# A four-batch transformer layer on one core: the instruction order of its 64 attention and feed-forward steps, and of the edges between batches, is changed

## The reference, cut to what matters

```
xn  = layernorm(x)
q, k, v = xn @ wq.T, xn @ wk.T, xn @ wv.T      # 8 heads, two maps (64 wide queries and keys) each
attn = softmax(causal(q1 k1)) - lambda * softmax(causal(q2 k2))
o   = attn @ v;  o = o * rsqrt(mean of o*o over groups of 8 + eps) * (1 - L_INIT);  att = o @ wo.T
h   = silu(xn @ W1.T) * (xn @ W3.T);  h = fwht(h);  ff = h @ W2.T
x   = x + att + ff                              # then layer 1: a recurrence and 64 routed experts
```

## Time and profile before

| | us |
|---|---|
| median of 3 runs | 3774.03 (3768.78 to 3781.55) |
| profiled execution: its time | 3770.78 |
| its span | 3769.0, mean granted clock 0.940 |
| PE busy | 3183.8 (84%) |
| DVE busy | 1951.8 (52%) |
| ACT busy | 1364.2 (36%) |
| POOL busy | 1859.7 (49%) |

### The profile page before, as it was taken

One profiled execution on the slowest core, in us unless ns is written; L12 is line 12 of the kernel. 1 busy time (PEld: TensorE's weight loads), 2 busy tenths in 40 slices (PEclk: granted clock), 3 DMA queues, 4 the chain that ended last, 5 costly groups with the idle time before them and its releaser, 6 DMA issues. The chain is left out here.

```text
span 3769.0 us, 46728 instructions
## 1 busy us (share of the span) xinstructions
PE 3183.8 (84%) x16049; PEld 2443.1 (65%) x16049; DVE 1951.8 (52%) x3951; ACT 1364.2 (36%) x2989; POOL 1859.7 (49%) x1707
## 2 busy tenths in 40 slices
PE   2899999899999979999989999995888983088776
PEld 0677777677777767777767777773776762044443
DVE  6355556645565655655664556565544655811110
ACT  2344444344444424444443444443323321022221
POOL 3256667646576645765773657654222241033333
PEclk9899999999999999999999999997998986589998
DMA  5211111321111141110123111103121111099897
GB/s 156 83 37 43 40 37 43 106 71 45 31 43 45 40 134 40 40 48 29 40 84 98 43 37 40 42 21 121 54 70 67 58 64 60 18 266 246 240 245 177
DMA packets 251183, 301.99 MB, mean 80 GB/s; under 512 B 19664, under 2 KB 168016, under 8 KB 250320
## 3 DMA queue, kind: packets, MB, share of 16 engines
q1 hardware_dynamic: 236624, 263.49, 22.3%
q0 software_dynamic: 14336, 35.66, 4.5%
HBM read 233.46 MB, written 65.57 MB: 79 GB/s over the span
## 5 line engine op out<-in xcount | busy, mean ns | idle before, releaser
L799 ACT ACTIVATE probs<-score_ps,neg_max 128x640 f32<-128x640 f32 (+7 forms) x512 | 374.4, 738 | 363.0 <-DVE neg_max L660 362.5
L690 POOL TENSOR_TENSOR probs<-probs 128x512 f32<-128x512 f32 (+3 forms) x384 | 383.4, 1013 | 10.7
L685 POOL TENSOR_SCALAR probs<-probs,comb 128x512 f32<-128x512 f32 (+3 forms) x384 | 230.0, 607 | 309.2 <-DVE comb L596 301.3
L660 DVE TENSOR_REDUCE neg_max<-score_ps 128x2 f32<-128x256 f32 (+7 forms) x256 | 346.5, 1353 | 58.9 <-PE score_ps L915 55.2
L694 POOL TENSOR_TENSOR out_root<-out_root,neg_half 128x16 f32<-128x16 f32 x128 | 371.8, 2907 | 5.7 <-DVE out_root L630 5.7
L552 DVE TENSOR_TENSOR layer_sum<-product_ps,layer_sum 128x512 f32<-128x512 f32 x384 | 262.4, 684 | 44.7 <-PE product_ps L61 41.6
L912 PE MATMUL score_ps<-keys_all,queries_all 64*128 64x512 f32 (+3 forms) x2304 | 277.2, 363 | 0.0
L539 DVE TENSOR_TENSOR attT<-turn_ps,attT 128x512 fp32r<-128x512 f32 (+3 forms) x384 | 211.6, 551 | 84.5 <-ACT attT L720 84.3
L720 ACT ACTIVATE attT<-turn_ps 128x512 fp32r<-128x512 f32 (+3 forms) x384 | 188.2, 490 | 142.8 <-PE turn_ps L825 142.8
L912 PEld LDWEIGHTS score_ps<-keys_all,queries_all 64*128 64x128 f32 x2304 | 187.8, 185 | 74.0 <-issue 44.7
L59 PE MATMUL product_ps<-xT_hi,w_up 128*128 128x512 f32 x512 | 211.6, 413 | 28.3 <-DVE queries_all L559 20.2
(11 more groups left out here) (248 smaller groups left out, 7676.3 us busy)
## 6 DMA issues: line engine op xcount, KB each, us to landing
e_gate_up<-in_w_gate_dram SPq DMA_DIRECT2D x64, 384.0 KB, 4.0
e_gate_up<-in_w_up_dram SPq DMA_DIRECT2D x64, 384.0 KB, 5.4
e_down<-in_w_down_dram SPq DMA_DIRECT2D x64, 384.0 KB, 6.8
w_stage<-in_wqk_dram SPq DMA_DIRECT2D x64, 256.0 KB, 3.1
w_stage<-in_w1T_dram SPq DMA_DIRECT2D x64, 256.0 KB, 2.6
w_stage<-in_w3T_dram SPq DMA_DIRECT2D x64, 256.0 KB, 2.7
values_by_head<-hidden_split SPq DMA_DIRECT2D x32, 512.0 KB, 3.2
w_stage<-w_transformed SPq DMA_DIRECT2D x64, 256.0 KB, 2.7
```

Source lines behind the costliest of these rows:

```text
L660: dve.tensor_reduce(nmax[:, i % 2, :], score_tile(i % NT), AX.X, ALU.max, negate=True)\
L685: pool.tensor_scalar(PR[:, r, 1, c], PR[:, r, 1, c], comb[:, i % 4:i % 4 + 1], 1.0, ALU.mult, ALU.mult)\
L690: pool.tensor_tensor(PR[:, r, 0, c], PR[:, r, 0, c], PR[:, r, 1, c], ALU.add).then_inc(s_comb, 1)
L799: act.activation(PR[:, i % 2, q, 0:(j + 1) * P], score_tile(j)[:, q, :], ACT.Exp, bias=nmax[:, i % 2, q:q + 1], accum_out=sums[:, i % 16, ...
```

## The change

It gives every engine a new order within a step, starts a batch's x earlier, and shortens the edges.

- TensorE: gate or up goes to the front of the step, ahead of values and the first turn; down goes from behind the scores to behind the turns; output goes ahead of projection (and so do their places in the bank order).
- ACT: tanh of gate goes to the front; the high part of a projection goes from the start of the next step, behind the weight copies, to directly behind this step's exponentials; the pair's high part goes behind the hidden tile's.
- DVE: output's sum goes to the front of the step, ahead of the projection's low part and the reciprocal; scaling of `heads_out` moves one step later, to its front; the factor of the normalised heads and the map's low part go behind gate or up; down's sum goes from the end of the step to before `comb`, and `comb` to directly before the pair's low part and the maximum.
- Edges: 11 slots instead of 13. Three tiles of x get a buffer of their own (`x_early`); they are loaded, and the first is prepared, in the last three steps of the batch before (slots -3 to -1, which run beside steps 61 to 63). Normalisation and statistics go to the end of a slot, transposes come in slots 1 to 8 (before 3 to 10), values in slots 2 to 9 (before 4 to 11).

```diff
-    HEAD_SLOTS, TAIL_SLOTS = 13, 10
+    HEAD_SLOTS, TAIL_SLOTS, EARLY = 11, 10, 3
+        XE = sb("x_early", [P, EARLY, D])
# phases()
-                for s in range(HEAD_SLOTS if b < batches else TAIL_SLOTS):
+                for s in range(0 if b else -EARLY, HEAD_SLOTS if b < batches else TAIL_SLOTS):
                     yield b - 1 if b else None, STEPS + s, b if b < batches else None, s
                 if b < batches:
                     for i in range(STEPS):
-                        yield b, i, None, None
+                        more = i >= STEPS - EARLY and b + 1 < batches
+                        yield b, i, b + 1 if more else None, i - STEPS if more else None
# SP
+                    if hb and s == -EARLY:
+                        sp.wait_ge(s_xtf, (hb - 1) * NT + EARLY)
+                        for t in range(EARLY):
+                            load_x(hb, t)
+                    if hb and s in (0, 1):
                         sp.wait_ge(s_ttf, tt[b, i, 1] + 1)
-                        for t in range(4 * s, 4 * s + 4):
+                        for t in range(EARLY + 4 * s, min(NT, EARLY + 4 * s + 4)):
                             load_x(hb, t)
# ACT
                     if b is not None:
-                        if proj_at(i - 1):
-                            proj_high(b, *proj_at(i - 1))
+                        if i < STEPS and i % 2 == 0:
+                            act.wait_ge(s_gbf, gb["GU", b, i] + 1)
+                            act.activation(sg[:, :], gbank("GU", b, i), ACT.Tanh, scale=0.5).then_inc(s_tanh, 1)
...
+                    if b is not None and proj_at(i):
+                        proj_high(b, *proj_at(i))
# TensorE
                     if b is not None:
+                        if i < STEPS:
+                            gate_up(b, i)
                         g = group_at(i)
                         if g is not None:
                             values(b, g)
                         if has_turn(i):
                             turn_map(b, i, 0)
-                    if hb is not None and 3 <= s < 3 + NT:
+                    if hb is not None and 1 <= s < 1 + NT:
...
-                        if i < STEPS:
-                            gate_up(b, i)
+                        if has_down(i):
+                            down(b, i)
...
-                        if has_down(i):
-                            down(b, i)
...
+                        if pair_at(i):
+                            output(b, i)
                         if proj_at(i):
                             project(b, *proj_at(i))
-                        if pair_at(i):
-                            output(b, i)
```

More of the change, by code:

```diff
@@ L612, in _ @@
-                        if has_turn(i):
-                            map_low(b, i, 0)
+                        g = group_at(i - 1) if i else None
+                        if g is not None:
+                            h = g // 4
+                            dve.wait_ge(s_ox, b * GROUPS + g + 1)
+                            if h % 2 == 0:
+                                at = (b, 16 * (h // 2) + g % 4 * 2 + 1, 2) if h else (b - 1, STEPS + g % 4 * 2 + 1, 2)
+                                if at[0] >= 0:
+                                    dve.wait_ge(s_ttf, tt[at] + 1)
+                            for q in range(2):
+                                tile = 2 * (g % 4) + q
+                                r = (h * NT + tile) % 16
+                                ins = dve.tensor_scalar(O[:, tile, h % 2 * DH:(h % 2 + 1) * DH],
+                                                        PV[:, 2 * P + q * DH:2 * P + (q + 1) * DH], rsum[:, r, 0:1], None, ALU.mult)
+                            ins.then_inc(s_oxf, 1)
@@ L749, in _ @@
                 for b, i, hb, s in phases():
-                    if hb is not None and 5 <= s < 5 + NT:
-                        t = s - 5
+                    if hb is not None and 3 <= s < 3 + NT:
+                        t = s - 3
                         act.wait_ge(s_vf, hb * NT + t + 1)
@@ L924, in _ @@
                             turn_map(b, i, 0)
-                    if hb is not None and 3 <= s < 3 + NT:
-                        t = s - 3
+                    if hb is not None and 1 <= s < 1 + NT:
+                        t = s - 1
                         pe.wait_ge(s_xn, hb * NT + t + 1)
```

164 lines of the change are left out of this document (76 added, 88 removed).

## The result

The changed kernel takes 3718.2 us (median of 4 runs, 3708.9 to 3721.6), the kernel before, measured beside it, 3774.6 (4 runs, 3768.8 to 3781.6). The ratio is 0.9846 with an interval of 0.9822 to 0.9870: 56 us, 1.5%, faster. The forecast was 3665 in a range of 3605 to 3735, so the time is inside the range, and the gain is about half of the 106 us that the sum gave.

The account below looks back on a forecast made before the run. TensorE's queue with a few holes was taken to bound the steps, chains the edges. Gains of 44 (steps), 37 (later edges) and 25 (first edge), 106 in all, took 3771 to 3665 us, range 3605 to 3735.

Parts of the forecast that it names:

- First edge, 25 us: Edge before the first batch: v(0) starts at about 93, slots of 3.4 instead of 6.86 us; gain 25 us.
- Later edges, 37 us: Three edges between batches: 74 us from the last maximum against 87.9, two slots dropped; gain 12.5 each, 37 in all.
- Last edge, 0 within 3: Edge after the last batch: slots stay at 3.6 us, down hides in that chain; change 0, within 3 us.
- Steps, 44 us: 64 steps in each of four batches: 25 - 11 - 3 = 11 us shorter, four times 44; bounds 0 and 100.
- 25 us of holes gone: Steps of a batch: TensorE's waits at values, up products and transposes, 18 to 25 us, taken as 25, all gained.
- 11 back at pair heads: New waits where pair heads start (fold, pair's transpose, later steps): 3.65 us for each of 3, 11 a batch.
- comb behind down's sum: In the steps: POOL's maps start later but keep 2.3 us of cover before the next turn; cost nothing.
- comb's holds, 3 a batch: In the 24 pair steps: comb held by a POOL copy beside it, between 0 and 1 us; 3 a batch.
- rival A: In the steps, holes only move: comb's holds and ACT's tanh cost all 25 us a batch; 3709 us, chance 0.24.
- C: In the steps, late comb makes a loop over POOL: 1.9 us for each of 96 pair steps, 182; 3891, chance 0.07.
- B: Edges bound by TensorE after slot 2 without clock loss, steps losing nearly all holes: 3594 us, chance 0.13.
- D: GpSimd's root holds the normalisation in edges (up to 2.4 us in 8 slots) and steps: 58 us, 3723, chance 0.03.

Follow-up runs that it names:

- Experiment 11: Changed kernel with comb directly behind the reciprocal and GpSimd's weight low parts in steps 15, 31, 47, 63 cut to 8 columns (work left out): 3664.5 us.
- experiment 1: Kernel before with only the changed edges, the order within steps left as before: 3722.7 us, ratio 0.9873.
- experiment 6: Changed kernel with comb directly behind the reciprocal and the mean again, ahead of down's sum: 3684.7 us, ratio 0.9766.
- experiment 5: Changed kernel with a projection's high part on ACT back at the start of the next step, behind the weight copies: 3722.7 us, ratio 0.9862.
- experiment 7: Changed kernel with GpSimd's weight low parts in steps 15, 31, 47, 63 cut to 8 of 512 columns, the rest left out: 3672.8 us.
- experiment 2: Changed kernel with 3 and 8 unread matmuls added before and behind the fold in steps 16, 32, 48: 3696.8 us, ratio 0.9803.
- experiment 8: Changed kernel with wo's piece at tile 4 of heads 1, 3, 5, tanh behind outT and map high, and DVE's factor, then map low first: 3744.2 us.
- experiment 3: Changed kernel with the output projection's weight piece handled at tile 4 of heads 1, 3, 5 instead of tile 7: 3684.5 us, ratio 0.9766.

## Why the prediction was half right

**What bounds the kernel: right.** TensorE's queue in the steps, chains in the edges. The holes named went away.

**First edge, 25 us: right (27.2).** v products start at 92.5, the first slot runs at half the pace until 96.5, and then slots come each 3.2 us (transposes at 100.46, 103.65, 106.86) against 6.86 before.

**Later edges, 37 us: right in kind, 30.1 measured.** Late slots with an output were put at 5.4 us; they take 5.32:

```profile
1318.74 0.60 PE L946 MATMUL score_ps<-ident_sb,probs 128*128 128x128 f32 x4
1318.84 2.91 POOL L705 TENSOR_TENSOR out_root<-out_root,neg_half 128x16 f32<-128x16 f32 x1
...
1320.09 0.28 DVE L618 SCALAR_TENSOR_TENSOR heads_out<-heads_out,out_root 128x128 f32<-128x128 f32 x1
...
1324.06 0.60 PE L946 MATMUL score_ps<-ident_sb,probs 128*128 128x128 f32 x4
```

The slots' sum gave 74 us from the last maximum. Experiment 11 has 74.5, at a clock of 0.98; the changed kernel has 77.7 to 79.3, at 0.89 in the row above, with stretches of 17.0 us at 1.2 GHz in the third edge where 3.4 are in experiment 11's. The term that failed is the 1.5 us "for clock at half in slots 0 and 1" with the waits in these slots; together they cost 3 to 5 us more per edge. How much of that is the clock was not run apart.

By stage the forecast asked for more than 37 here and for less in the steps: down of step 63, 1.4 us, moves into the steps (354 matmuls of down between the first and the last scores of a batch, 348 before). So by stage the forecast is 88 to 74 us an edge, 41.7 us in three, of which 30.1 came, and 38.4 us in the steps.

**Last edge, 0 within 3: wrong, 4.7 us longer.** With the old order of a step and the new edges it takes 41.6 us (experiment 1), so the new order makes it longer; with `comb` early it takes 43.6 (experiment 6). The rest is open.

**Steps, 44 us: wrong, 2.9 us longer instead.** This is the step of the prediction that failed, and its largest term. By its own terms:
- *25 us of holes gone.* The waits at up products and values went, as said. But by experiment 5 the eviction's place gives only 1 us in a head without pairs: the output ahead of the projection and gate or up in front had done the rest.
- *11 back at pair heads.* The chain was right (fold 0.5: measured 0.52; second turn 0.75: 0.48; pair 0.9: 0.72 in experiment 7). It left out that the factor, 0.28 us, can be held like `comb`; it took 1.39. The prediction had the row of a held `comb` (1.15 us) and applied it only to `comb`. The two copies that step 15 leaves behind the hidden one on GpSimd were passed over with "POOL's halves follow, used a step later: nothing". That sentence is the one that failed: the copies' results are used late, but while they run they hold VectorE.
- *comb behind down's sum: "nothing".* It cost 28 us (experiment 6); with the copies short it still costs 11.5 (experiment 11), of which the steps' part is the hidden copy's hold in steps 20 and 22 of a pair head and the same places of the others. 2.3 us of cover for maps was counted, and was enough; not that a later root shifts the copies onto the factor.
- *comb's holds, 3 a batch.* They were not found: of 63 in the steps of the second batch none lasts over 0.59 us, and half of them 0.21 or less.
- *Clock in the steps: not in the sum at all.* "in the steps, where TensorE is never idle long, it stays at 2.4 GHz" was true of before. The sum itself put 2.15 us of waits into one step, and did not ask what that does to the clock. By experiment 2: 21 us.

With `comb` back at its place and these copies short, experiment 11 has first maximum 27.3, edges 41.4 and steps 37.8 us better than before: 106.5 by the last maximum, against 25 + 37 + 44 = 106. So close an agreement is partly luck: work is left out there, one part of the change is undone, four stretches at 1.2 GHz and the hold in step 23 are left beside the first pair head's. It shows that the two effects missed, the held factor and the clock, are as large as the difference, and proves no term.

That the time lies in the range is luck in part as well: the range reached down to the time without any gain in the steps because rival A had it so, for another reason. The bounds of its terms (steps 0 and 100, an edge 5 and 22, the first 6 and 28) also span 3577 to 3750, and not the 3620 to 3705 that it gives.

**The rivals.** A came nearest, 3709 against 3718, and had the mechanism in part: a hold eats the steps' gain, but that of the factor, not of `comb`, and the clock with it; tanh's part is the fold's wait, 1.7 us a batch. C had its first links right, a late `comb` making GpSimd's root late, but not the loop: 28 us of 182, paid through held factors. B's steps did not come. D is refuted by the rows of the late slot above: GpSimd's root runs from 1318.84 to 1321.75, and the factor, two inputs in SBUF, takes its free 0.28 us in the midst of it, at 1320.09. The Trainium skill (SBUF — State Buffer, "SBUF: two separate sides") lets a GpSimd instruction that reads SBUF keep the shared port pair, if it starts first, for its whole length against a VectorE instruction with two SBUF inputs. The trace agrees for each subtraction of GpSimd met here (1.39, 1.34, 1.05, 0.85 us); it does not agree for the root. `out_root`'s tensor_scalar at 866.41, beside a copy, took 0.33 instead of 0.17 us.

**Not settled.** What the edges lose to the clock and what to waits, what tanh's place costs by itself, and most of the last edge's 4.7 us. An order in which the factor meets no copy at all, with all work done, was not tried.

## What to carry to other kernels

When instructions that read SBUF twice are moved on VectorE, write down which GpSimd instruction runs at their new place, as one writes down semaphores: here 0.28 us became 1.39 us on the path in some steps, and no wait in the program shows it. Don't put such an instruction directly behind a wait for GpSimd if GpSimd's next instruction is a copy (1344 ns in the median of experiment 8). And when a change gathers several small waits of TensorE into one step, price the clock too; if the wait can't go, unread matmuls in it may pay for themselves (21 us here).

## What the runs showed of the hardware that was not expected

- In the changed kernel TensorE's gaps of 0.5 and 1.8 us behind each other, in a stretch that otherwise ran at 2.4 GHz, were followed by 3.4 or 6.8 us at 1.2 GHz at all twelve pair-head beginnings. Shorter gaps did not always spare it: with 0.5, 0.7 and 0.3 us none of eleven such beginnings had one in experiment 7, but four of eleven in experiment 11 (with 1.1 and 0.5 us five of twelve in experiment 3).
- A held factor ends 0.15 us behind GpSimd's copy (864.17 + 1.27 and 864.20 + 1.39). In the 14 traces together 567 factors began with more than 0.25 us of a subtraction of GpSimd left, and every one ended 0.14 to 0.15 us behind it. An instruction that reads PSUM and SBUF isn't held (the map's low part at 865.51, beside the copy of 865.39, takes 0.68 us, as it does elsewhere).
- GpSimd's longest instruction, the root (2.91 us), did not hold the factor or, in the earlier trace rows, the normalisation; its copies of 1.3 us hold. In the 14 traces 221 factors began with more than 0.25 us of such a root left, and 144 so beside a scale of the maps by `comb`: all took 0.27 to 0.30 us.
